# How often attention and norm work is driven between the matmul groups of the output projection: paces 6 and 1 become 3 and 3

## The chip, the cores and the metric

The kernel runs on one Trainium2 chip, as one program on 8 cores. Each core takes 2048 of the 16384 tokens and the whole of every weight matrix; the cores exchange nothing. The metric is the device time of the slowest core in microseconds.

## What is computed

One transformer layer on x of 16384 tokens x 4096. Attention is over the heads of one token: for each token 64 queries, 64 keys and 64 values of width 64 give a 64 x 64 score matrix. The second part is a matmul with bias plus a mixture of 8 rank-16 experts, the top two per token.

```python
def attn(h):                      # h: layernorm(x)
    q, k, v = (h @ W.T).reshape(b, s, 64, 64)       # for Wq, Wk, Wv; q, k, v times head-dim masks
    w = softmax(einsum('bshd,bsgd->bshg', q, k) / 8)
    return einsum('bshg,bsgd->bshd', w, v).reshape(b, s, 4096) @ Wo.T
def ffn(h):
    base = h @ W_base.T + b_base
    rw, sel = top_k(h @ W_router.T, 2); w = onehot-sum of softmax(rw) at sel
    return base + 2 * einsum('ter,te,eor->to', einsum('td,erd->ter', h, A), w, B)
x = x + layernorm(attn(layernorm(x)))
x = x + layernorm(ffn(layernorm(x)))
```

## The kernel before

Each engine's instruction list is written out by hand: a Python function `emit` appends an instruction to one of five lists (tensor, vector, scalar, gpsimd, sync) with the semaphore values it waits for. Each engine works its list strictly in the order in which Python emitted it. DMAs are instructions too: those on the sync list stand on SP's queue, those on the gpsimd list on POOL's, and a DMA that waits holds up all that is behind it on that list.

A core's 2048 tokens are two chunks (`c` = 0, 1) of 1024, and a chunk is eight slices of 128 tokens (`tau`). The transposed activations of a chunk stand in LNT. A projection of a chunk goes over eight blocks of 512 output columns (`n`), each block over eight groups (`ktg`). A group is one weight load of 128 x 2048 bf16 (512 KB, one of four buffers WG) and its matmuls of 128 x 128 by 128 x 512, four per slice. In a half projection with four slices a group has 16 matmuls. After a block, ACT copies the four banks out of PSUM (L601) and POOL writes them to DRAM (apn).

Weights come in two ways. In chunk 0 the first use of a matrix is "cast_save": POOL loads float32 with a cast (1 MB read), and SP then writes the bf16 form to a scratch tensor; the buffer is free for the fourth group after when that save has landed and the matmuls are done. All other uses are "scratch": SP loads the bf16 form (WG<-s_wo).

The stages of a chunk are: layer norm and transposes; the projections q, k, v (written to DRAM); attention for slices 0 to 3, on its own; then the two halves of the wo projection, which the change touches:

- First half (`proj_half` on slices 0 to 3), with the generator `a3_units` for the attention of slices 4 to 7. A slice has two batches of 64 tokens. A batch (`attn_batch`) has one unit that issues eight gathers on SP with 128-byte pieces (QSG, KB, VB), then four waves of six units (Q transposes; K transposes with the QBD copies on DVE; scores with the KTS copies on ACT; maximum, exponentials and P transposes; output matmuls with QBD copies on ACT; normalization into OB on DVE), then one unit that issues the two writes of OB to DRAM on SP. After both batches one unit issues the read-back BFN<-on on POOL, and one transposes BFN into LNT (L278). These are 2 x 26 + 2 = 54 units per slice and 216 in all.
- Second half (`proj_half` on slices 4 to 7, weights from scratch), with the generator `a5_b0_units` for slices 0 to 3. A slice has six units: load of T2 and XT on POOL and a layer norm; the residual add, the xp write and a second layer norm; transposes of BFN; the 32 router matmuls; the top-2 arithmetic on DVE; one matmul and a copy of the router weights (L677, L680). These are 24 units.

After the matmuls of every group `drive(gen, pace)` takes `pace` units from the generator, if it has any, and so puts their instructions behind that group on every list. After the last block `drain` takes what is left with no group between. Then come the rest of the same layer-norm work with the expert part, and the second matrix in two halves.

Of the kernel before, what the change touches and what calls it, by code (L numbers as in the profile page):

```python
# [26 lines left out]
def _build_program():  # L27
# [25 lines left out]
    ap_d = nc.dram_tensor("apn", [CH, DM], F32, kind="Internal").ap()  # L53
# [67 lines left out]
    def emit(eng, fn, waits=(), inc=None, amt=1):  # L121
        w = []
        for s_, v_ in waits:
            assert v_ <= cnt[s_], f"{eng}: wait on future {s_}={v_}>{cnt[s_]}"
            if v_ > seen[eng][s_]:
                seen[eng][s_] = v_
                w.append((s_, v_))
        if inc is not None:
            cnt[inc] += amt
        sched[eng].append((tuple(w), fn, inc, amt))  # L130
        return cnt[inc] if inc is not None else None
# [3 lines left out]
    def g_w(*keys):  # L135
        out = []
        for k in keys:
            out += guards.get(k, [])
        return out

    def g_set(key, *pairs):
        guards[key] = list(pairs)
# [4 lines left out]
    def dma(eng, out, in_, waits=(), sem=None):  # L147
        return emit(eng, lambda e, o=out, i=in_: e.dma_start(out=o, in_=i),  # L148
                    waits, inc=sem, amt=16)
# [90 lines left out]
    def load_wgroup(nm, n, ktg, kind):  # L240
        b = wg_idx[0] % 4
        wg_idx[0] += 1
        waits = g_w(f"WG{b}")
        if kind == "cast_save":
            src = wT[nm].rearrange("(a p) c -> a p c", p=128)[
                4 * ktg:4 * ktg + 4, :, 512 * n:512 * n + 512].transpose([1, 0, 2])
            uv = dma("gpsimd", WG[b][:].rearrange("p (a c) -> p a c", a=4), src, waits,
                     sem=f"wgu{b}")
            rdy = (f"wgu{b}", uv)
            qv = dma("sync", wS[nm][n, ktg], WG[b][:], [rdy], sem=f"sw{b}")  # L250
            g_set(f"WG{b}", (f"sw{b}", qv))
        else:
            rdy = (f"wg{b}", dma("sync", WG[b][:], wS[nm][n, ktg], waits, sem=f"wg{b}"))
            g_set(f"WG{b}")
        return b, rdy

    def wg_done(b, sem, val):
        g_add(f"WG{b}", (sem, val))
# [38 lines left out]
    for c in range(NCH):  # L297
      try:
# [257 lines left out]
        def drive(gen, k):  # L556
            for _ in range(k):
                if next(gen, "END") == "END":
                    return False
            return True  # L560

        def drain(gen):
            for _ in gen:
                pass
# [3 lines left out]
        a35h0_v, a35h0_s = cnt["V"], cnt["S"]  # L568
# [1 line left out]
        ph(4, c)  # L570
        ap_i = [0]

        def proj_half(nm, taus, banks, src, gen, img_d, first_waits=(), pace=3):
            for n in range(NB):
                for ktg in range(8):
                    b, rdy = load_wgroup(nm, n, ktg, src)
                    for k4 in range(4):
                        kt = ktg * 4 + k4
                        for ti, tau in enumerate(taus):
                            waits = []  # L580
                            if k4 == 0 and ti == 0:
                                waits.append(rdy)
                            if ktg == 0 and k4 == 0:
                                waits += g_w(f"bank{banks[ti]}")
                                if n == 0 and ti == 0:
                                    waits += list(first_waits)
                            emit("tensor",
                                 lambda e, kt=kt, tau=tau, b=b, k4=k4, bk=banks[ti],
                                        st=(ktg == 0 and k4 == 0), sp=(ktg == 7 and k4 == 3):
                                 e.matmul(pb(bk, 0, 512),  # L590
                                          LNT[:, colk(kt, tau):colk(kt, tau) + 128],
                                          WG[b][:, k4 * 512:k4 * 512 + 512], start=st, stop=sp),
                                 waits, inc="T" if (k4 == 3 and ti == len(taus) - 1) else None)
                    wg_done(b, "T", cnt["T"])
                    if gen is not None:
                        drive(gen, pace)
                tmm = cnt["T"]
                for ti, tau in enumerate(taus):
                    sl = ap_i[0] % 4
                    ap_i[0] += 1  # L600
                    ev = emit("scalar", lambda e, bk=banks[ti], sl=sl: e.activation(  # L601
                        APST[:, sl * 512:sl * 512 + 512], pb(bk, 0, 512), AF.Copy),
                        ([("T", tmm)] if ti == 0 else []) + g_w(f"APs{sl}"), inc="S")
                    g_set(f"bank{banks[ti]}", ("S", ev))
                    uv = dma("gpsimd", img_d[tau * 128:tau * 128 + 128, 512 * n:512 * n + 512],
                             APST[:, sl * 512:sl * 512 + 512], [("S", ev)], sem=f"ap{sl}")
                    g_set(f"APs{sl}", (f"ap{sl}", uv))

        gen_h1 = a3_units(range(4, 8), 8, (4, 5, 6, 7))
        proj_half("wo", [0, 1, 2, 3], [0, 1, 2, 3], src_kind0, gen_h1, ap_d,  # L610
                  [("V", a35h0_v), ("S", a35h0_s)], pace=6)
        drain(gen_h1)
        g_set("LNTa", ("T", cnt["T"]))
        a4h0_ap = [(f"ap{i}", cnt[f"ap{i}"]) for i in range(4)]
        a4h0_vs = [("V", cnt["V"]), ("S", cnt["S"])]

        def a5_b0_units(taus, tbank):
            for tau in taus:
# [22 lines left out]
                for kt in range(KT):  # L641
# [43 lines left out]

        gen_a5h0 = a5_b0_units(range(0, 4), (0, 1, 2, 3))
        a4h1_ap = [None]
        proj_half("wo", [4, 5, 6, 7], [4, 5, 6, 7], "scratch", gen_a5h0, ap_d, a4h0_vs,
                  pace=1)
        a4h1_ap[0] = [(f"ap{i}", cnt[f"ap{i}"]) for i in range(4)]  # L690
        drain(gen_a5h0)
        g_set("LNTb", ("T", cnt["T"]))
# [188 lines left out]
```

How the kernel before makes its waits and increments, by code:

```python
        def run(eng):  # L827
            for waits, fn, inc, amt in sched[name]:
                for s_, v_ in waits:
                    eng.wait_ge(sems[s_], v_)
                instr = fn(eng)
                if inc is not None:
                    instr.then_inc(sems[inc], amt)
```

## Time and profile before

| | us |
|---|---|
| median of the two timed runs | 8399.7 (8324.7 and 8474.7) |
| the profiled execution, its own time | 8290.5 |
| its span, slowest core (core 2) | 8288.9 |
| spans of the eight cores | 8245.5 to 8288.9 |
| TensorE matmul busy | 5459.9 (66%) |
| DVE busy | 1493.0 (18%) |
| ACT busy | 773.5 (9%) |

The time of one execution is the span of its slowest core plus the little that lies around it, 1.6 us here. Busy time of TensorE counts the matmuls as the trace models them: they are pipelined, so the start of one to the start of the next says more than a duration. The chain that ended last consists for 57% of TensorE, 17% of DMA, 11% of DVE and 6% of ACT work. The mean granted TensorE clock is 0.81 of full speed, as a mean over time at the two levels of 1.2 and 2.4 GHz.

### The profile page before, as it was taken

To read this page: it belongs to the slowest core of one execution; us is meant where nothing else is said; L and a number is where in the kernel's file an instruction comes from. 1 tells how busy PE (TensorE), PEld (TensorE's weight loads), DVE (VectorE), ACT (ScalarE), POOL (GpSimd) and SP (SyncE) were. 2 spreads that over 40 slices of the span, in tenths; PEclk is the share of its full clock that TensorE was granted. 3 is DMA by queue.
4 is the path that set the end of the run, shared out by engine and by line. 5 is a ranking of instruction groups with operands and counts; after the bars stand their busy time and mean duration, and the time that the engine had idled before them with its cause. 6 is when DMAs were issued, how large, how long until landed. Compare 5 with 4: busy or idle time off the path is not lost.

```text
span 8288.9 us, 69958 instructions; the slowest of 8 cores (8245.5 to 8288.9 us)
## 1 busy us (share of the span) xinstructions
PE 5459.9 (66%) x28056; PEld 2571.1 (31%) x28056; DVE 1493.0 (18%) x2144; ACT 773.5 (9%) x1427; POOL 498.9 (6%) x785
## 2 busy tenths in 40 slices
PE   4888888842344568465736888888842556676964
PEld 2333333322222223122313333333322223332321
DVE  4000000023212131401033000000023221414012
ACT  1000000012211100000001000000012221000000
POOL 1000000000000110111100000000000000000110
PEclk7999999965666789688868999999965677887977
DMA  6666666632454675698552222222223334655655
GB/s 148 143 144 141 144 140 140 143 71 51 84 100 96 133 222 177 184 195 225 178 207 89 79 80 82 77 76 76 78 54 54 82 79 113 224 171 172 206 187 190
DMA packets 940079, 1084.79 MB, mean 131 GB/s; under 512 B 575217, under 2 KB 792306, under 8 KB 923378
## 3 DMA queue, kind: packets, MB, share of 16 engines
q0 software_dynamic: 225872, 492.98, 26.3%
q1 hardware_dynamic: 713890, 587.34, 23.4%
q8 instruction: 229, 3.75, 0.2%
q14 instruction: 88, 0.72, 0.0%
HBM read 885.23 MB, written 369.10 MB: 151 GB/s over the span
## 4 chain that ended last, share of the span: by engine, by line
PE 57%; DMA 17%; DVE 11%; ACT 6%; SPq 4%; issue 4%; POOL 1%; DVEq 0%; ACTq 0%; POOLq 0%
PE PALL L341 33%; PE PALL L590 10%; PE PALL L764 8%; SPq L148 4%; DVE BN L192 4%; DMA WG<-wbT 3%; DMA T<-yn 2%; DMA WG<-woT 2%; DMA VB<-vn 2%; ACT QBD L494 2%; ACT PSTG L470 2%; PE PALL L278 1%; DMA T<-apn 1%; PE PALL L487 1%; PE PALL L407 1%
## 5 line engine op out<-in xcount | busy, mean ns | idle before, releaser
L341 PE MATMUL PALL<-WG,LNT 128*128 128x512 bf16 x12288 | 2798.9, 390 | 411.4 <-DVE QST L359 112.7
L341 PEld LDWEIGHTS PALL<-WG,LNT 128*128 128x128 bf16 x12288 | 1224.7, 100 | 1985.1 <-issue 623.0
L590 PE MATMUL PALL<-WG,LNT 128*128 128x512 bf16 x4096 | 1081.4, 428 | 166.2 <-DMA WG<-woT 106.7
L764 PE MATMUL PALL<-WG,LNT 128*128 128x512 bf16 x4096 | 935.1, 390 | 158.3 <-DMA WG<-wbT 146.8
L278 PE MATMUL PALL<-idt,BFN 128*128 128x128 bf16 x1536 | 165.9, 304 | 783.8 <-DVE BFN L204 556.4
L590 PEld LDWEIGHTS PALL<-WG,LNT 128*128 128x128 bf16 x4096 | 434.3, 108 | 772.5 <-issue 421.8
L764 PEld LDWEIGHTS PALL<-WG,LNT 128*128 128x128 bf16 x4096 | 404.5, 100 | 678.4 <-issue 237.0
L192 DVE BATCH_NORM_STATS2 BN<-T 128x6 f32<-128x512 f32 x320 | 193.6, 676 | 1914.5 <-DMA T<-yn 1262.9
L359 DVE TENSOR_TENSOR QST<-PALL,maskK 128x512 bf16<-128x512 f32 x128 | 81.3, 685 | 2067.9 <-PE PALL L341 2022.5
L278 PEld LDWEIGHTS PALL<-idt,BFN 128*128 128x128 bf16 x1536 | 154.8, 143 | 796.1 <-issue 795.0
L435 ACT ACTIVATE KTS<-PALL 128x512 bf16<-128x512 f32 x192 | 104.2, 595 | 2960.2 <-PE PALL L427 2960.2
L407 PE MATMUL PALL<-idt,QSG 128*128 128x128 bf16 x1024 | 104.4, 274 | 402.9 <-DMA VB<-vn 374.3
L416 DVE CAST QBD<-PALL 128x512 bf16<-128x512 f32 x256 | 162.0, 685 | 629.7 <-PE PALL L407 629.7
L359 DVE TENSOR_TENSOR QST<-PALL,maskV 128x512 bf16<-128x512 f32 x128 | 81.0, 685 | 990.8 <-PE PALL L341 950.6
L487 PE MATMUL PALL<-idt,PSTG 128*128 128x128 bf16 x1024 | 104.5, 274 | 219.6 <-ACT PSTG L470 219.6
L407 PEld LDWEIGHTS PALL<-idt,QSG 128*128 128x128 bf16 x1024 | 88.3, 126 | 421.2 <-issue 415.3
L470 ACT ACTIVATE PSTG<-PALL,NM 64x512 bf16<-64x512 f32 x256 | 167.6, 679 | 212.9 <-DVE NM L461 122.0
L481 DVE TENSOR_REDUCE ZW<-PSTG 128x8 f32<-128x1024 bf16 (+1 forms) x96 | 151.3, 1576 | 199.6 <-ACT PSTG L470 199.6
L290 DVE CAST LNT<-PALL 128x512 bf16<-128x512 f32 x192 | 132.3, 692 | 285.9 <-PE PALL L278 285.5
L148 POOL DMA_DIRECT2D BFN<-on x16 | 8.6, 536 | 2763.1 <-DMA on<-OB 2718.1
L777 PE MATMUL PALL<-bbn,onesb 1*128 1x512 bf16 x128 | 51.4, 401 | 186.6 <-DMA bbn<-bb 186.6
L786 ACT ACTIVATE APST<-PALL 128x512 f32<-128x512 f32 x128 | 76.2, 597 | 1035.2 <-PE PALL L781 1031.2
(99 smaller groups left out, 2166.7 us busy)
## 6 DMA issues: line engine op xcount, KB each, us to landing
WG<-s_wo SPq DMA_DIRECT2D x192, 512.0 KB, 3.9
WG<-s_wb SPq DMA_DIRECT2D x192, 512.0 KB, 3.6
XT<-x POOLq DMA_DIRECT2D x24, 2048.0 KB, 12.3
WG<-wqT POOLq DMA_DIRECT2D x64, 512.0 KB, 5.7
s_wq<-WG SPq DMA_DIRECT2D x64, 512.0 KB, 2.8
WG<-wkT POOLq DMA_DIRECT2D x64, 512.0 KB, 5.7
s_wk<-WG SPq DMA_DIRECT2D x64, 512.0 KB, 3.1
WG<-wvT POOLq DMA_DIRECT2D x64, 512.0 KB, 5.7
```

The lines of the kernel that those rows point to most:

```text
L148: return emit(eng, lambda e, o=out, i=in_: e.dma_start(out=o, in_=i), waits, inc=sem, amt=16)
L192: emit("vector", lambda e, i=i: e.bn_stats(BN[:, 6 * i:6 * i + 6], src_ap[:, 512 * i:512 * i + 512]), (list(vwaits) + g_w("MV") + g_w("BN" ...
L278: emit("tensor", lambda e, bk=bk, kt=kt, off=off: e.matmul(pb(bk, off * 128, 128), src_sb[:, kt * 128:kt * 128 + 128], idt[:], start=True, ...
L341: e.matmul(pb(tau, 0, 512), LNT[:, colk(kt, tau):colk(kt, tau) + 128], WG[b][:, k4 * 512:k4 * 512 + 512], start=st, stop=sp),
L359: ev = emit("vector", lambda e, tau=tau, sl=sl, mk=mk: e.tensor_tensor(QST[:, sl * 512:sl * 512 + 512].rearrange("p (h d) -> p h d", d=64) ...
L407: emit("tensor", lambda e, j=j, jj=jj, p=p, qb_bk=qb_bk: e.matmul(pb(qb_bk[j // 4], (j % 4) * 128, 128), QSG[p][:, jj * 128:jj * 128 + 128 ...
L416: emit("vector", lambda e, pw=pw, bk=bk, i_=i_: e.tensor_copy(QBD[pw][:, i_ * 512:i_ * 512 + 512], pb(bk, 0, 512)), [("T", t_s0)] if i_ == ...
L470: s_s6 = emit("scalar", lambda e, a=a, pw=pw, bk_i=bk_i, sb_=s_bk[bk_i]: e.activation(PSTG[pw][64 * a:64 * a + 64, bk_i * 1024:bk_i * 1024 ...
L487: emit("tensor", lambda e, j=j, pw=pw, ptb=pt_bk[j // 4], po=(j % 4) * 128: e.matmul(pb(ptb, po, 128), PSTG[pw][:, j * 128:j * 128 + 128], ...
L494: emit("scalar", lambda e, pw=pw, bk=bk, i_=i_: e.activation(QBD[pw][:, i_ * 512:i_ * 512 + 512], pb(bk, 0, 512), AF.Copy), [("T", t_s7)] ...
L590: e.matmul(pb(bk, 0, 512), LNT[:, colk(kt, tau):colk(kt, tau) + 128], WG[b][:, k4 * 512:k4 * 512 + 512], start=st, stop=sp),
L764: e.matmul(pb(bk, 0, 512), LNT[:, colk(kt, tau):colk(kt, tau) + 128], WG[b][:, k4 * 512:k4 * 512 + 512], start=st, stop=False), waits,
```

## The change

Two numbers change. In the first half of the wo projection, three attention units are driven after each group and no longer six. In the second half, three norm and router units are driven after each group and no longer one. The parameter `pace` is gone, and the 3 that was its default is written in place. No instruction is added or removed; their order on the engines' lists is another.

```diff
-        def proj_half(nm, taus, banks, src, gen, img_d, first_waits=(), pace=3):
+        def proj_half(nm, taus, banks, src, gen, img_d, first_waits=()):
...
                     if gen is not None:
-                        drive(gen, pace)
+                        drive(gen, 3)
...
         proj_half("wo", [0, 1, 2, 3], [0, 1, 2, 3], src_kind0, gen_h1, ap_d,
-                  [("V", a35h0_v), ("S", a35h0_s)], pace=6)
+                  [("V", a35h0_v), ("S", a35h0_s)])
...
-        proj_half("wo", [4, 5, 6, 7], [4, 5, 6, 7], "scratch", gen_a5h0, ap_d, a4h0_vs,
-                  pace=1)
+        proj_half("wo", [4, 5, 6, 7], [4, 5, 6, 7], "scratch", gen_a5h0, ap_d, a4h0_vs)
```

## Rows read from the trace of the kernel before

**Rows 1.** Stretches: busy us (instructions) per engine, granted clock, DMA share, GB/s.

```profile
2139.00:2811.00 672.00, 292.91 (x1984) 150.15 (x1984) 142.02 (x208) 130.32 (x224) 37.81 (x56) 0.67 0.48 94
2811.00:2976.00 165.00, 109.36 (x450) 45.15 (x451) 0.11 (x1) 8.68 (x17) 25.90 (x39) 0.86 0.95 201
2976.00:3307.00 331.00, 248.87 (x1283) 115.88 (x1281) 99.92 (x160) 29.00 (x64) 23.45 (x42) 0.88 0.57 199
6466.00:6994.00 528.00, 287.44 (x1985) 147.74 (x1986) 141.58 (x208) 130.19 (x224) 10.69 (x20) 0.72 0.35 85
6994.00:7100.00 106.00, 99.94 (x452) 43.97 (x451) 0.57 (x1) 8.86 (x18) 7.82 (x15) 0.99 0.52 168
7100.00:7427.00 327.00, 247.64 (x1284) 115.93 (x1281) 99.91 (x160) 29.00 (x64) 23.38 (x42) 0.87 0.61 205
```

**Rows 2.** Timeline, TensorE, chunk 1, first batch: start, duration, instruction, idle before.

```profile
6498.16 0.61 PE L407 MATMUL PALL<-idt,QSG 128*128 128x128 bf16 x8
...
6500.42 0.39 PE L446 MATMUL PALL<-KTS,QBD 128*128 128x64 bf16 x8 [1.43 <-ACT KTS L435]
6503.23 0.61 PE L487 MATMUL PALL<-idt,PSTG 128*128 128x128 bf16 x8 [2.41 <-ACT PSTG L470]
...
6505.56 6.27 PE L590 MATMUL PALL<-WG,LNT 128*128 128x512 bf16 x16
```

**Rows 3.** Timeline, TensorE, chunk 1, second half: eight groups of one block.

```profile
7280.29 28.61 PE L590 MATMUL PALL<-WG,LNT 128*128 128x512 bf16 x128 [0.89 <-ACT APST L601]
```

**Rows 4.** Groups by line, TensorE, 6466 to 6994: busy us, mean ns, idle before.

```profile
L590 PE MATMUL PALL<-WG,LNT 128*128 128x512 bf16 x577 | 201.9, 524 | 4.4 <-ACT APST L601 3.6 <-ACT LNT L292 0.8
...
L278 PE MATMUL PALL<-idt,BFN 128*128 128x128 bf16 x128 | 14.3, 310 | 55.0 <-DMA BFN<-on 55.0
```

**Rows 5.** Timeline, TensorE, chunk 1, second batch: the Q transposes.

```profile
6557.60 0.61 PE L407 MATMUL PALL<-idt,QSG 128*128 128x128 bf16 x8 [1.12 <-DVE OB L520]
```

**Rows 6.** Timeline, chunk 1, TensorE and SP's queue, where a slice begins.

```profile
6598.42 4.24 PE L590 MATMUL PALL<-WG,LNT 128*128 128x512 bf16 x16
...
6600.08 2.98 SPq L148 DMA_DIRECT2D WG<-s_wo  x4
```

**Rows 7.** Second batch's load: SP's queue, landing of its WG loads, TensorE's Q.

```profile
6520.19 1.63 SPq L148 DMA_DIRECT2D on<-OB  x2
...
6531.91 2.71 SPq L148 DMA_DIRECT2D WG<-s_wo  x4
...
DMA to landing us min/median/max: 5.5/5.9/7.0
...
6535.13 1.01 PE L407 MATMUL PALL<-idt,QSG 128*128 128x128 bf16 x8 [9.72 <-DMA VB<-vn]
```

**Rows 8.** Timeline, TensorE: groups right after a short gap, chunk 0 and chunk 1.

```profile
2960.16 8.75 PE L590 MATMUL PALL<-WG,LNT 128*128 128x512 bf16 x32 [2.58 <-DMA WG<-woT]
...
7099.64 10.52 PE L590 MATMUL PALL<-WG,LNT 128*128 128x512 bf16 x48 [2.36 <-ACT APST L601]
```

**Rows 9.** Timeline, TensorE, chunk 0: first load, block's end, second load.

```profile
2164.47 1.01 PE L407 MATMUL PALL<-idt,QSG 128*128 128x128 bf16 x8 [21.21 <-DMA VB<-vn]
...
2280.71 5.83 PE L590 MATMUL PALL<-WG,LNT 128*128 128x512 bf16 x16 [11.51 <-DMA WG<-woT]
...
2399.84 1.01 PE L407 MATMUL PALL<-idt,QSG 128*128 128x128 bf16 x8 [11.42 <-DMA VB<-vn]
```

**Rows 10.** Timeline, chunk 1, second half and just behind it: TensorE, then DVE.

```profile
7141.69 3.57 PE L278 MATMUL PALL<-idt,BFN 128*128 128x128 bf16 x32 [31.53 <-DVE BFN L204]
...
7263.80 3.57 PE L278 MATMUL PALL<-idt,BFN 128*128 128x128 bf16 x32 [14.19 <-DVE BFN L204]
...
7476.61 0.27 PE L677 MATMUL PALL<-idt,WBF 128*8 128x128 bf16 x1 [3.52 <-DVE WBF L672]
...
7157.23 4.83 DVE L192 BATCH_NORM_STATS2 BN<-T 128x6 f32<-128x512 f32 x8
...
7177.18 2.41 DVE L204 TENSOR_SCALAR BFN<-XT,NMR,RSTD 128x4096 bf16<-128x4096 f32 x1
```

## The prediction, made before the changed kernel had run

> **What bounds the kernel now.** I read the stretches first [rows 1]. A chunk has two stretches that the edit touches: the first half of the wo projection, with attention units driven between its matmul groups, and the second half, with the layer-norm and router units driven between them. In chunk 0 these are 672 + 165 = 837 us and 331 us; in chunk 1, 528 + 106 = 634 us and 327 us. That is 2129 of 8289 us, and only these can move directly. TensorE is the engine to watch: it takes all of this work in one order, and every stall sits in its queue. In the attention part it is busy about half the time at a granted clock of 0.67 to 0.72; afterwards, with groups alone, it is busy 0.99 of the time in chunk 1 with DVE idle, and in chunk 0 the DMA engines are at 0.95 of their time. So in chunk 0 the leftover groups wait for weights, in chunk 1 they run at full speed, and no group is left to cover an attention stall.
>
> Then I read TensorE's own order of instructions in chunk 1 [rows 2]. One wave of attention is five steps, Q and K transposes, scores S, P transposes, output O. With pace 6 one group stands between O and the next Q. The stalls are 1.43 us before S, 2.41 before P, 1.33 before O: Q's start to the next group's start is 6505.56 - 6498.16 = 7.4 us. Groups are long too. 16 matmuls take 28.61 / 8 = 3.6 us at the 2.4 GHz level [rows 3], but 6.27 in the row shown, and 201.9 / 36 = 5.6 in the mean of the stretch's 36 [rows 4]. They start at the lower clock after the wave. In a slice's second batch the group falls between S and P, which hides the 2.41, but leaves 1.33, 1.12 (Q on DVE's OB) and 1.43 [rows 2, 5].
>
> **What the first edit does.** A slice of attention has 54 units: 26 for each batch (a load unit, four waves of six, a write unit) and two for reading the result back. Four slices are 216. Pace 6 spends them in 36 groups and leaves 28 bare. Pace 3 puts 18 groups in each slice, 192 units in 64 groups, and 24 units (last slice, from P of its fifth wave on) are drained with no group. Place by place, per slice, first in chunk 1:
>
> First batch, units 2 to 25. After Q and K comes a group, then S P O, then a group. The 1.43 before S is hidden. S to the next group's start is 6505.56 - 6500.42 = 5.1 us. Q and K take 0.9 with nothing to wait for. The group after Q and K follows straight on a running one, so 3.6; the group after S P O follows 3.7 us of stalls in 5.1, and I keep 5.6. Sum: first group 4.2 [rows 6], Q and K 0.9 + 0.5 wait, second group 3.6, four times (5.1 + 5.6) = 42.8, three times (0.9 + 3.6) = 13.5: 65.5.
>
> Second batch. Its output writes and loads stand on SP's queue, and the next weight loads behind them. SP begins at 6520.19, issues 12 us of writes and gathers, gets to the weights at 6531.91 and these land 5.9 later, at 6537.8. The Q transposes at 6535.13 waited 9.72 for the gathers after a group of 6.3 [rows 7], so O ended at 6519.1 and the weights come 18.7 after it. Now the next group stands behind S, just in time. At pace 3 the units 25 to 27 hold no TensorE work, so two groups stand there, but the second one's weights are the ones behind the gathers: it can't start before 18.7. The wait is 18.7 - 5.6 = 13.1, that group 5.6 after the pause; the edit makes this place worse by 3. The same at the first load of a slice: those weights are issued at 6600.08 and come about 6606, where Q and K would end at 6604.2 (6598.42 + 4.24 + 0.5 + 0.9) [rows 6], a wait of 1.8. The rest is dense: Q K S is 6500.42 + 0.39 - 6498.16 = 2.65, P O is 6505.56 - 6503.23 = 2.3, four of each 19.8, and eight groups. Between them lie only gaps of 1.3 to 1.4 us. For the clock the rows say: three groups after a gap of 2.36 us ran at 10.52 = 3.5 each, two after 2.58 us at 8.75 = 4.4 each [rows 8]. So gaps of 1.4 keep the upper level; I take 3.6, with 2.0 once for warming: 30.8. TensorE waits 55.0 / 4 = 13.7 us for a slice's read-back after O [rows 4], of which the group after unit 51 hides 3.6: 10.1; the transposes take 3.4. Sum with the 1.8: 13.1 + 5.6 + 19.8 + 30.8 + 10.1 + 3.4 + 1.8 = 84.6.
>
> A slice is 150 us. Three are 450; the last runs to unit 30, 65.5 + 1.8 + 13.1 + 5.6 + 2.65 = 88.7. The drain: P and O 4.9, three waves of 7.4 + 1.2, read-back 13.7 + 3.4: 47.8. Total 587 against 634: **47 us saved**. Nine groups more per slice cost 18 us there, against 33 us bare.
>
> Chunk 0 differs in that weights come by POOL with a cast and are saved by SP [rows 9]. The gathers wait for that save, so Q waits 21.2 at a slice's start and its next group starts cold (5.6). The second batch's Q waits 11.42 after a group of 6.4, so it starts 17.8 after O; here both groups have their weights already, so 17.8 - 5.6 - 3.6 = 8.6. A block's end costs 11.5 to 13.9, since the next weights stand behind the result writes on POOL; there are seven, and they stay seven: one of them, after the eighth group, now falls on the gathers' wait and I count 7 for it, 12 for the others. A slice: 4.2 + 21.2 + 1.4 (Q and K at the lower clock) + 5.6 + 42.8 + 13.5 = 88.7; then 8.6 + 3.6 + 11.3 (three times 2.65, once 3.3) + 9.3 + 30.8 + 10.4 + 5 (transposes and the weights behind the read-back) = 79. Three are 503; block ends 67 + 12; last slice 88.7 + 8.6 + 3.6 + 3.3 = 104; drain 48; small waits for weights in the dense part 10. Total 744 against 837: **93 saved**. Most is the 165 us of bare groups at 5.9 each, paced by DMA, which go behind attention. DMA work allows it: 0.48 x 672 / 4 = 81 us per slice, plus nine groups at 0.95 x 165 / 28 = 5.6, gives 131 of about 184 us.
>
> The Trainium skill (DMA: Bandwidth & Descriptors, Issuing engines are not separate DMA queues) says that transfers from all issuing engines run on the same 16 DMA engines and interleave. By that, the doubled weight traffic lengthens the gathers. The rows bear it out mildly: gathers are ready 17.8 us after O in chunk 0 with cast loads beside them, about 16 in chunk 1. If each of the two gathers of a slice took 2 us more, the sum would lose 14 us a chunk.
>
> **What the second edit does.** A slice has 6 units, four slices 24. Pace 1 spreads them over 24 groups, pace 3 over 8. The transposes wait for a DVE chain: two layer norms and an add, 7157.23 to 7179.6, 22.4 us [rows 10]. Now slices are 7263.80 - 7141.69 = 122.1 over three, 40.7 each, since three groups lie between the transposes and the next chain's start on DVE. At pace 3 that is 3.4 transposes, a group 3.6, router matmuls about 1, a bare wait for the router weights 3.5, then 0.6: 12.1, and with 22.6 for the chain 34.7. The first chain starts earlier: the last result writes have landed during the drain, and the T2 load is issued right behind the read-back, so I put the first transposes 26 us after the stage's start where they stand 42 after it now (7099.64 to 7141.69). Total 26 + 3 x 34.7 + 12.1 + seven blocks of 29.5 = 348.7 against 327: **21 lost** in each chunk. Bounds: with the chain period unchanged and no earlier start, 16 groups uncovered, 59; with PE-side savings complete, 10.
>
> **Sum.** 47 + 93 - 42 = 98 saved: 8290.5 - 98 = 8193. This is against the profiled execution's own time; the two timed runs stand 0.4% and 2.2% above it (8324.7 and 8474.7, median 8399.7).
>
> **The rivals.** *The clock stays down between the groups.* If the eight dense groups and the four after Q and K ran at 5.6 too, each costs 2.0 more: 12 x 2.0 x 3.5 slices x 2 chunks = 168 lost, hence 8193 + 168 = 8361, slower than before. For it: every one of the 36 groups now starts below full speed after stalls of 1.1 to 2.4 us. Against: those stalls add up to 3.9 us or more before a group, and here to 1.4. It decides at 98 / 84 = 1.2 us per group, a mean of 4.8 us in these places. *The clock stays up everywhere.* If the groups after S P O also run at 3.6, 4 x 2.0 x 3.5 x 2 = 56 more saved, 8137. For it: the low stretch shrinks from 7.4 us with Q and K to 5.1; in the row shown P still runs at the upper level. *The second edit pays in full.* 59 instead of 21 in each chunk: 8269. For it, ACT's evacuation of a block stands behind the chain; against, now all units end inside the first block. *Weights run short in chunk 0.* The bare groups' 5.9 us for 64 groups and 27 us of attention transfers per slice make a floor of 486 us, well under 744; only the small waits could grow, to some 30 us: 8213, which I count to the forecast.
>
> **How the numbers follow.** Forecast (8193, own range 8160 to 8230) 0.5; clock up everywhere 0.2; second edit in full 0.12; clock down 0.1; rest, spread either way, 0.08. The range 8080 to 8320 takes in 8137 with as much again, 8269 and half of the clock rival, and leaves out the rest. Two per cent, about what a measurement of this kernel can tell from no change, is 166 us. Faster by more needs the warm rival and something more, 0.15; slower by more needs the cold one and something more, 0.04; the same 0.81.
>
> **What would show it.** Right: between 2.4 GHz groups the stretch from Q K to the next group shows groups of 3.6; a second-batch group waits about 13 us for WG from s_wo in chunk 1, just after O; the first half lasts 740 to 750 us in chunk 0 and 580 to 590 in chunk 1; 24 units run without a group at its end; all router work lies in the first 8 groups of the second half, 34.7 us apart, then 29.5 us blocks; the second half 345 to 352. Wrong: dense groups at over 4.8 us, gathers that take over 20 us, or a first transposition in the second half that still comes 40 us in.

## The result, and the profile after

The change makes the kernel 1.0% faster: the ratio of its time to that of the kernel before is 0.9897, with a 95% interval of 0.9882 to 0.9911. By the measure of 2% that is no change, as forecast; the 86 us that the ratio stands for compare with the 98 of the sum. The median over all 12 executions is 8387.5 us against 8403.4 before: in seven of the 12 (8321.5 to 8777.8 us) one or both dies ran TensorE at a lower granted clock, as happens to the kernel before too, and all other times here are of the other executions, or of cores on a die to which this did not happen. The profiled execution took 8229.8 us (8290.5 before), its slowest core was core 7.

The four stretches that answer to [rows 1] are these, in the same columns (start and end in the span, length, busy us of TensorE, weight loads, DVE, ACT and POOL, granted clock, DMA share, GB/s):

```profile
2139.00:2890.00 751.00, 367.53 (x2434) 187.59 (x2435) 142.03 (x208) 139.01 (x240) 65.47 (x98) 0.73 0.66 135
2890.00:3235.00 345.00, 252.53 (x1284) 117.77 (x1281) 99.96 (x160) 29.40 (x65) 20.25 (x38) 0.86 0.51 178
6407.00:7006.00 599.00, 358.78 (x2432) 181.62 (x2430) 142.03 (x208) 138.88 (x240) 20.30 (x38) 0.80 0.41 110
7006.00:7355.00 349.00, 253.74 (x1284) 118.81 (x1284) 99.96 (x160) 29.73 (x66) 20.22 (x38) 0.86 0.54 182
```

| stretch | before | by the prediction | after |
|---|---|---|---|
| chunk 0, first half | 837 | 744 | 751 |
| chunk 0, second half | 331 | 352 | 345 |
| chunk 1, first half | 634 | 587 | 599 |
| chunk 1, second half | 327 | 349 | 349 |
| together | 2129 | 2032 | 2044 |

So 85 us are gained in these stretches: 121 in the first halves, 36 given back in the second. The granted clock of the first halves rose a little: before it was 0.67 and 0.86 in the two parts of chunk 0, 0.71 as a mean over time, and 0.72 and 0.99 in those of chunk 1, 0.77 as a mean; now it is 0.73 and 0.80. No part with bare groups is left in them. The spans of the two traces differ by 61 us and not by 85, since the rest of the program took 24 us longer here. Nor is one core all cores: in this same execution the first half of chunk 0 lasts 733 to 751 us from core to core and that of chunk 1 587 to 603, and core 7 is at or near the upper end of both. (The half is taken here from its first group to the first group behind its last read-back.)

TensorE's timeline in chunk 1, first batch and then second batch, answers to [rows 2] and [rows 5] (start, duration, instruction, idle before and who ended it):

```profile
6441.56 3.63 PE L590 MATMUL PALL<-WG,LNT 128*128 128x512 bf16 x16
...
6447.84 0.61 PE L487 MATMUL PALL<-idt,PSTG 128*128 128x128 bf16 x8 [2.41 <-ACT PSTG L470]
6449.77 0.59 PE L506 MATMUL PALL<-VB,QBD 128*128 128x64 bf16 x8 [1.33 <-ACT QBD L494]
6450.17 6.33 PE L590 MATMUL PALL<-WG,LNT 128*128 128x512 bf16 x16
...
6488.36 5.99 PE L590 MATMUL PALL<-WG,LNT 128*128 128x512 bf16 x16 [15.04 <-DMA WG<-s_wo]
...
6496.45 0.39 PE L446 MATMUL PALL<-KTS,QBD 128*128 128x64 bf16 x8 [1.43 <-ACT KTS L435]
6496.68 3.62 PE L590 MATMUL PALL<-WG,LNT 128*128 128x512 bf16 x16
...
6502.07 0.39 PE L506 MATMUL PALL<-VB,QBD 128*128 128x64 bf16 x8 [1.33 <-ACT QBD L494]
6502.30 3.62 PE L590 MATMUL PALL<-WG,LNT 128*128 128x512 bf16 x16
...
6531.14 0.39 PE L446 MATMUL PALL<-KTS,QBD 128*128 128x64 bf16 x8 [1.43 <-ACT KTS L435]
6532.43 6.12 PE L590 MATMUL PALL<-WG,LNT 128*128 128x512 bf16 x16 [0.89 <-ACT APST L601]
```

The group after Q and K takes 3.63 us, the one after S P O still 4.8 to 6.3. In the second batch six groups in a row take 3.62, though a gap of 1.33 or 1.43 us stands before and behind each. The two exceptions there are the group behind the long wait (5.99) and the one that begins a block: ACT's copies out of PSUM put a second gap of 0.89 us behind the 1.43 before S, and it takes 6.12. The one long wait is for weights, 15.04 us in the middle of the slice, as the queue order of [rows 7] had it. SP's queue at that place:

```profile
6466.64 2.90 SPq L148 DMA_DIRECT2D on<-OB  x2
6469.59 6.11 SPq L148 DMA_DIRECT2D QSG<-qn  x2
...
6482.95 11.79 SPq L148 DMA_DIRECT2D WG<-s_wo  x5
```

The weights are issued 16.3 us after the writes of OB, behind eight gathers. In chunk 0 the rows that answer to [rows 9], TensorE first and then SP's queue between its second and third row:

```profile
2164.28 1.01 PE L407 MATMUL PALL<-idt,QSG 128*128 128x128 bf16 x8 [21.60 <-DMA VB<-vn]
...
2234.30 9.97 PE L590 MATMUL PALL<-WG,LNT 128*128 128x512 bf16 x32 [13.92 <-DMA WG<-woT]
2264.31 1.01 PE L407 MATMUL PALL<-idt,QSG 128*128 128x128 bf16 x8 [20.04 <-DMA VB<-vn]
```

```profile
2234.12 0.32 SPq L148 DMA_DIRECT2D s_wo<-WG  x1
2234.53 9.06 SPq L148 DMA_DIRECT2D on<-OB  x2
2243.68 7.71 SPq L148 DMA_DIRECT2D QSG<-qn  x2
```

And in chunk 1's second half, for [rows 10], the first two transposes and the first block without units:

```profile
7031.25 3.57 PE L278 MATMUL PALL<-idt,BFN 128*128 128x128 bf16 x32 [21.36 <-DVE BFN L204]
...
7066.27 3.57 PE L278 MATMUL PALL<-idt,BFN 128*128 128x128 bf16 x32 [17.90 <-DVE BFN L204]
...
7147.54 30.06 PE L590 MATMUL PALL<-WG,LNT 128*128 128x512 bf16 x128 [0.89 <-ACT APST L601]
```

The transposes come 25 us after the half's start at 7006.3 and the next lie 35.0 us later, as worked out (26 and 34.7).

### The profile page after: what moved, and what is told of

Its sections match the earlier page's. It is cut to its first block, busy times and chain, and to the rows that moved or that the text cites. A ratio compares the mean times of both kernels' runs of the same rounds, so it can differ in the third digit from the quotient of the medians.

```text
span 8228.2 us, 69958 instructions; the slowest of 8 cores (8151.4 to 8228.2 us)
## 1 busy us (share of the span) xinstructions
PE 5400.6 (66%) x28056; PEld 2555.5 (31%) x28056; DVE 1491.4 (18%) x2144; ACT 774.2 (9%) x1427; POOL 496.2 (6%) x785
## 4 chain that ended last, share of the span: by engine, by line
PE 58%; DMA 15%; DVE 11%; ACT 6%; SPq 5%; issue 4%; POOL 1%; DVEq 0%; ACTq 0%; POOLq 0%
PE PALL L341 33%; PE PALL L590 11%; PE PALL L763 8%; SPq L148 5%; DVE BN L192 4%; DMA WG<-wbT 3%; DMA T<-yn 3%; ACT QBD L494 2%; ACT PSTG L470 2%; DMA VB<-vn 1%; PE PALL L278 1%; PE PALL L487 1%; DMA WG<-woT 1%; PE PALL L407 1%; DMA T<-apn 1%
## 5 line engine op out<-in xcount | busy, mean ns | idle before, releaser
L590 PE MATMUL PALL<-WG,LNT 128*128 128x512 bf16 x4096 | 1040.2, 415 | 182.5 <-DMA WG<-woT 93.3
```

The source lines that it names most:

```text
L590: e.matmul(pb(bk, 0, 512), LNT[:, colk(kt, tau):colk(kt, tau) + 128], WG[b][:, k4 * 512:k4 * 512 + 512], start=st, stop=sp),
```

## The experiments

All edits are shown against the kernel before, with the parts left out marked by `...`. From the third experiment on the paces are 3 and 3, as in the changed kernel, where nothing else is said.

**Each edit alone.** The theory says that they pull against each other. The first edit alone:

```diff
-                  [("V", a35h0_v), ("S", a35h0_s)], pace=6)
+                  [("V", a35h0_v), ("S", a35h0_s)], pace=3)
```

> Pace 3 in the first half, 1 in the second. Theory (the stage sums of the changed kernel's trace: first halves 85 and 34 us shorter, second halves 14 and 21 longer, of which the earlier start of the norm chain already gives back some 16 in each): the first halves as in the changed kernel, about 750 and 600 us, and the second halves 313 us each instead of 331 and 327, since transposes come 28 us in instead of 42. Together 147 us less than before, ratio 0.982. Rival (the second halves are untouched by the first edit; the drain gives them nothing): 119 us less, ratio 0.986, second halves 331 and 327.

It took 8162.7 us where the kernel before took 8304.8 and 8314.7 on the same chip: 0.982, from one execution. The windows of core 6 in the traced execution, which is another one, first and second half of each chunk:

```profile
2135.00:2870.00 735.00, 365.33 (x2432) 187.16 (x2432) 142.14 (x209) 139.00 (x241) 65.50 (x98) 0.73 0.65 137
2870.00:3179.00 309.00, 250.34 (x1284) 116.52 (x1284) 99.98 (x161) 29.36 (x65) 21.62 (x38) 0.90 0.58 200
6328.00:6940.00 612.00, 365.10 (x2432) 183.35 (x2430) 141.93 (x208) 138.67 (x240) 20.31 (x38) 0.79 0.41 108
6940.00:7251.00 311.00, 247.52 (x1284) 115.73 (x1284) 100.11 (x161) 29.50 (x66) 21.60 (x38) 0.91 0.60 204
```

The second halves take 309 and 311 us with pace 1, less than the 331 and 327 before: the first edit's drain gives them a head start for the norm chain. The rival, that they are untouched, falls. The first halves show how far one core of one trace can be trusted: 735 and 612 here where the same code in the changed kernel had 751 and 599.

The second edit alone:

```diff
         proj_half("wo", [4, 5, 6, 7], [4, 5, 6, 7], "scratch", gen_a5h0, ap_d, a4h0_vs,
-                  pace=1)
+                  pace=3)
```

> Pace 6 in the first half, 3 in the second. Theory: without the drain in front the first transposes come 42 us in, then three slices of 34.4, 12 and seven blocks of 29.5: 364 us where it was 327 to 331, so 35 us lost in each chunk, 70 in all, ratio 1.0085, and the first halves unchanged at 837 and 634. Rival (all 16 groups bare at 3.7): 59 in each, ratio 1.014.

It took 8386.8 us, 1.009 of before, one execution again. TensorE's timeline, start of chunk 1's second half:

```profile
7099.47 3.61 PE L590 MATMUL PALL<-WG,LNT 128*128 128x512 bf16 x16 [2.36 <-ACT APST L601]
7136.27 3.23 PE L278 MATMUL PALL<-idt,BFN 128*128 128x128 bf16 x32 [33.19 <-DVE BFN L204]
```

One group and then 33 us of waiting, where before three groups lay ahead of the transposes. From 7099.5 to the half's end at 7457.7 are 358 us, 31 more than before; in chunk 0 it is 364, 33 more. The theory's 35 holds, the rival's 59 doesn't. On these whole times, one execution each, the first edit is worth about 147 us and the second costs about 77, of which 64 lie in the two second halves of the core shown; together 70, near the 86 measured for both.

**Where the mid-slice wait comes from.** The load of the next group is put on SP's queue before the units driven after this one, in the halves with scratch weights.

```diff
-                    b, rdy = load_wgroup(nm, n, ktg, src)
+                    b, rdy = nxt if nxt is not None else load_wgroup(nm, n, ktg, src)
...
                     wg_done(b, "T", cnt["T"])
+                    nxt = None
+                    if src == "scratch" and gen is not None and n * 8 + ktg < 63:
+                        nxt = load_wgroup(nm, (n * 8 + ktg + 1) // 8, (ktg + 1) % 8, src)
                     if gen is not None:
                         drive(gen, pace)
```

> Paces 3 and 3; where weights come by SP from scratch, the load of the next group is put on SP's queue before the units driven after this group, and no longer behind them. It touches the first half of chunk 1 and the second halves. Theory (the 13 to 15 us wait for WG in the middle of a slice is the place behind the gathers on SP's queue): the wait moves to the Q transposes and shrinks to about 7 us after two groups, the second group of a slice waits for nothing; some 11 us per slice, chunk 1's first half from 599 to about 562, ratio about 0.985 against before. Rival (the weights are late because the DMA engines are busy with the gathers, wherever they stand): chunk 1's first half stays within 8 us of 599, ratio 0.990.

Measured: 8211.2 us, 0.988 of before. TensorE's timeline on core 0, chunk 1, the place where core 7 of the changed kernel waited 15.04 us:

```profile
6484.79 9.76 PE L591 MATMUL PALL<-WG,LNT 128*128 128x512 bf16 x32 [0.89 <-ACT APST L605]
6503.70 1.01 PE L407 MATMUL PALL<-idt,QSG 128*128 128x128 bf16 x8 [9.16 <-DMA VB<-vn]
```

Both groups now run together, and Q waits 9.16 (about 7 expected). The first half of chunk 1 takes 564 us on this core and 560 to 572 over all eight, where the changed kernel had 587 to 603: core by core 22 to 39 us less, 30 in the mean, against the 37 of the theory and the 8 at most of the rival. The order on the queue made the wait; the weights themselves are there in time beside the gathers. The whole kernel gained some 20 us on the changed one (0.985 of before was expected), from a single execution.

**What the clock level is worth.** A slice is cut so that the groups fall after S and after O in both batches.

```diff
-                        drive(gen, pace)
+                        drive(gen, pace[(n * 8 + ktg) % len(pace)] if isinstance(pace, list) else pace)
...
-                  [("V", a35h0_v), ("S", a35h0_s)], pace=6)
+                  [("V", a35h0_v), ("S", a35h0_s)],
+                  pace=[4] + [3] * 7 + [5] + [3] * 8)
```

> Paces 3 and 3, but in the first half a slice is cut 4, seven times 3, 5, eight times 3, so that in both batches the groups fall after S and after O. Theory (the clock level between the groups is worth as much as the stalls that they hide): all groups but those after a gather or read-back wait run at 3.6 us; chunk 1's first half from 599 to about 540, chunk 0's from 750 to about 720; ratio 0.979. Rival (only stalls count, groups after S P O gain nothing when S stands before them): about 4 us per slice, 15 per chunk, ratio 0.986.

> The kernel of aligned once more, for a trace on an undisturbed die: by the clock theory chunk 1's first half is about 540 us with groups after S and after O at 3.6 us in both batches; by the rival about 585 with the groups of the first batch at 5 us.

It took 8167.6 and, in the second run, 8124.9 us: 0.983 and 0.980 of before. The trace of the second run, core 3: first its windows of the first halves, then a stretch of chunk 1's first batch.

```profile
2135.00:2870.00 735.00, 342.19 (x2433) 178.31 (x2434) 142.14 (x208) 139.04 (x240) 65.51 (x98) 0.74 0.66 136
6368.00:6907.00 539.00, 331.20 (x2434) 173.19 (x2432) 142.15 (x208) 139.06 (x240) 20.32 (x38) 0.84 0.46 123
```

```profile
6445.16 0.39 PE L506 MATMUL PALL<-VB,QBD 128*128 128x64 bf16 x8 [1.33 <-ACT QBD L494]
6445.47 3.61 PE L590 MATMUL PALL<-WG,LNT 128*128 128x512 bf16 x16
...
6451.18 0.39 PE L446 MATMUL PALL<-KTS,QBD 128*128 128x64 bf16 x8 [1.43 <-ACT KTS L435]
6451.41 3.62 PE L590 MATMUL PALL<-WG,LNT 128*128 128x512 bf16 x16
```

Chunk 1's first half is 539 us (540 expected; 527 to 539 over all cores), and the groups take 3.6 except those that begin a block or follow a pause (up to 6.2). To see how the 60 us divide, the groups by line of chunk 1's first half: first the changed kernel, then this one.

```profile
L590 PE MATMUL PALL<-WG,LNT 128*128 128x512 bf16 x1024 | 282.6, 436 | 70.1 <-DMA WG<-s_wo 62.7 <-ACT APST L601 6.2 <-ACT LNT L292 0.8
L487 PE MATMUL PALL<-idt,PSTG 128*128 128x128 bf16 x256 | 21.5, 232 | 49.9 <-ACT PSTG L470 49.9
L407 PE MATMUL PALL<-idt,QSG 128*128 128x128 bf16 x256 | 20.7, 227 | 5.1 <-DVE OB L520 3.5 <-DMA VB<-vn 1.4 <-PE PALL L590 0.2
...
L446 PE MATMUL PALL<-KTS,QBD 128*128 128x64 bf16 x256 | 13.2, 197 | 22.8 <-ACT KTS L435 22.8
```

```profile
L590 PE MATMUL PALL<-WG,LNT 128*128 128x512 bf16 x1024 | 258.3, 407 | 9.7 <-ACT APST L601 6.3 <-DMA WG<-s_wo 1.1 <-ACT LNT L292 0.8
L407 PE MATMUL PALL<-idt,QSG 128*128 128x128 bf16 x256 | 21.5, 233 | 55.4 <-DMA VB<-vn 53.8 <-DVE OB L520 1.1 <-PE PALL L590 0.4
L487 PE MATMUL PALL<-idt,PSTG 128*128 128x128 bf16 x256 | 20.3, 224 | 6.2 <-ACT PSTG L470 6.2
...
L446 PE MATMUL PALL<-KTS,QBD 128*128 128x64 bf16 x256 | 13.7, 200 | 45.5 <-ACT KTS L435 45.5
```

The groups themselves give 24 us (282.6 to 258.3), which is clock; the wait before P gives 44 and the one before S takes back 23; the mid-slice wait only changes its name from WG to VB, 62.7 to 53.8. So the clock is worth about as much as the hidden stalls, and the rival, which allowed 15 us, falls.

In chunk 0 the theory failed: 735 us on this core and not 720, and over all cores 730 to 738 where the changed kernel already had 733 to 751, 5 us less in the mean. The Q transposes there, first in the changed kernel and then in this one:

```profile
L407 PE MATMUL PALL<-idt,QSG 128*128 128x128 bf16 x256 | 23.9, 249 | 125.7 <-DMA VB<-vn 122.3 <-DVE OB L520 3.4
L407 PE MATMUL PALL<-idt,QSG 128*128 128x128 bf16 x256 | 23.1, 243 | 164.1 <-DMA VB<-vn 163.0 <-DVE OB L520 1.1
```

TensorE saved the same things as in chunk 1 (19 us in the groups, 44 before P, less 23 before S), and the wait for gathers grew by 41: the gathers came no earlier, so TensorE only stood longer in front of them.

**Chunk 0.** The save of a group's weights is put behind the driven units on SP's queue.

```diff
+                    late = [] if gen is not None else None
+                    b, rdy = load_wgroup(nm, n, ktg, src, late)
...
                     if gen is not None:
                         drive(gen, pace)
+                    for sv in late or []:
+                        sv()
```

> Paces 3 and 3; in chunk 0's first half the save of a group's weights is put on SP's queue behind the units driven after the group and no longer ahead of them. Theory (at a slice's start the Q transposes wait 22, 22, 17 and 9 us since the gathers stand on SP behind a save that waits for weights which POOL could only ask for after the read-back): these four waits go to under 5 us each, the ones in the middle of a slice from 20 and 15 to about 8, and chunk 0's first half goes from 750 to about 670. Rival (the gathers are slow in chunk 0 because cast loads share the DMA engines): the waits stay within 3 us of what they are, 750 stays.

By what was said with the result, this kernel has no whole time to compare, only cores of its trace. On core 5 the first half of chunk 0 takes 703 us (670 expected; the same core had 742 in the changed kernel). The four waits of Q at a slice's start are 10.4, 12.7, 9.6 and 5.9 us where they were 21.6, 22.4, 16.9 and 9.2, and the first two in a slice's middle 11.9 and 11.3 where they were 20.0 and 15.1. All Q waits for gathers together make 77.4 us where core 7 of the changed kernel had 122.3; core 7 of this run has 71.2 and also 703 us. So the order on the queue was some 40% of it, more than the rival allows and less than the theory said. Part of the remainder is SP's own issuing. SP's queue around the first gathers, first here and then in the changed kernel:

```profile
2118.45 4.42 SPq L148 DMA_DIRECT2D QSG<-qn  x2
2122.97 22.74 SPq L148 DMA_DIRECT2D KB<-kn  x4
```

```profile
2138.91 9.55 SPq L148 DMA_DIRECT2D QSG<-qn  x2
2148.56 8.74 SPq L148 DMA_DIRECT2D KB<-kn  x4
```

Started early, the gathers stand beside the read-back and the four cast loads behind it, and issuing the four KB gathers takes SP 22.74 us instead of 8.74. So the rival has its part too.

**Weights three groups ahead.** Both halves ask for weights three groups ahead of the matmuls, and the saves stand behind the driven units. `prefetch(k)` puts all loads up to group k on their queues and keeps their saves in a list.

```diff
+            prefetch(3)
...
-                    b, rdy = load_wgroup(nm, n, ktg, src)
+                    b, rdy = wq_[n * 8 + ktg]
...
                     wg_done(b, "T", cnt["T"])
+                    prefetch(n * 8 + ktg + 3)
                     if gen is not None:
                         drive(gen, pace)
+                    if saves[n * 8 + ktg] is not None:
+                        saves[n * 8 + ktg]()
```

> Paces 3 and 3; both halves ask for weights three groups ahead of the matmuls, and saves stand behind the driven units. Theory (in chunk 0 the seven block ends cost 13 us each because the next weights stand behind the result writes on POOL, and the mid-slice waits come from SP's order): chunk 0's first half from 750 to 570 to 600 us, chunk 1's from 599 to about 555, ratio about 0.966. Rival (chunk 0 is bound by the DMA engines themselves, so waits only move): chunk 0's first half not under 680, ratio 0.98 or more.

It took 8028.3 to 8059.6 us in three executions against 8291.5 and 8293.8: 0.971, from 0.968 to 0.972 over all pairs. The group of the matmuls in chunk 0's first half (2133 to 2753 on core 1, 620 us):

```profile
L607 PE MATMUL PALL<-WG,LNT 128*128 128x512 bf16 x1027 | 280.3, 433 | 9.2 <-ACT APST L621 6.2 <-DMA WG<-woT 1.4 <-ACT LNT L299 0.8
```

The wait for woT is 1.4 us where the changed kernel had 93.3: the waits at block ends came of loading too late, behind the result writes on POOL, and are gone. 620 (614 to 624 over all cores) is above the 570 to 600 expected, since 75 us of waits for gathers remain. Chunk 1 has 568 (555 expected), no less than with weights one group ahead.

**All of it.** Weights three groups ahead, late saves, the gathers of a batch issued one batch ahead (in the attention stage without groups too), the cut of the aligned kernel, and pace 1 in the second half. The edit beyond those shown is in the batch generator:

```diff
+            if (tau, bt) == ahead[0]:
+                issue_gathers(tau, bt)
+            nx = ahead.index((tau, bt)) + 1
+            if nx < len(ahead):
+                issue_gathers(*ahead[nx])
```

> Weights three groups ahead and late saves; gathers of a batch issued one batch ahead, in both attention stages; the first half cut 4, seven times 3, 5, eight times 3; pace 1 in the second half. Theory (stalls before Q are queue order, the clock stays up when S stands before the group, pace 1 covers the norm chain): chunk 1's first half about 480 us, chunk 0's about 510, second halves about 312, the attention stage without groups some 70 us shorter per chunk; ratio 0.92 to 0.94. Rival (transfers collide once nothing waits, the read-back and the weights take longer): first halves above 560 each, ratio 0.95 or more.

It took 7641.1 to 7653.5 us in three executions against 8291.5 and 8293.8: 0.922, from 0.921 to 0.923 over all pairs. The windows of core 3:

```profile
2056.00:2602.00 546.00, 326.83 (x2432) 171.41 (x2432) 142.13 (x208) 139.10 (x241) 65.41 (x98) 0.84 0.90 182
2602.00:2913.00 311.00, 249.24 (x1284) 116.09 (x1284) 99.92 (x160) 29.02 (x64) 21.62 (x38) 0.89 0.57 200
6006.00:6468.00 462.00, 307.15 (x2433) 166.35 (x2434) 142.14 (x208) 139.07 (x240) 20.31 (x38) 0.92 0.54 140
6468.00:6777.00 309.00, 246.11 (x1284) 115.11 (x1282) 99.91 (x160) 29.00 (x64) 21.59 (x38) 0.91 0.58 205
```

Chunk 1's first half takes 462 us (480 expected), chunk 0's 546 (510 expected): there the DMA engines are at 0.90 of their time, which points at the transfers as the next limit, though no run tests that. Of the 645 us gained, 501 lie in these stretches (2129 to 1628). The rest lies outside them: the attention stage ahead of the first half now ends 79 us earlier in chunk 0 (at 2056 against 2135 on the same core of the aligned kernel).

## Why the prediction was right or wrong

*The mechanism and its size were right.* Faster by about 1%, inside 2%, with 93 and 47 us gained and 42 given back: measured 86 (837 - 751), 35, and 36. The likeliest case was the one that came.

*The step that failed is the base on which the number and its range stand.* "This is against the profiled execution's own time; the two timed runs stand 0.4% and 2.2% above it". I saw the two, put what stands above the profiled execution at nothing, and drew 8080 to 8320 from the bounds of the costs alone. The median of all executions, 8387.5, lies outside it, 194 us above the 8193. Of these, some 154 are the reason given with the result, of which the 8474.7 was a sign: the five executions that it leaves are at 8230 to 8237, inside the range. The other 40 are about 29 of base and 12 of gain: the five like executions of the kernel before have a median of 8319 and not the 8290.5 of its profiled one, and 86 us were gained and not 98. The spread of the measurement belonged into the range as a term of its own.

*First edit, chunk 1.* Term by term: slices of 153, 150 and 150 us where 150 was the sum. The group behind the gathers waited 15.0, 13.7, 15.4 and 13.6 us (13.1), the second group of a slice 1.4 to 1.9 (1.8). Dense groups were 3.62 (3.6). The step that was short is the drain. "three waves of 7.4 + 1.2" was taken from waves that follow a group; without groups every instruction ran at the lower clock (eight Q transposes took 1.01 us and not 0.61), and a wave took 9.8 us (Q to Q, 6958.89 to 6968.70). The 12 us by which 599 exceeds 587 are 9 from the last slice and 3 from the first. Of the 9 the three waves are 3 to 4; the rest are the first P of the drain, which waited 3.8 us and not 2.4, a read-back wait of 15.0 and not 13.7, and small pieces.

*First edit, chunk 0.* The step that failed is "one of them, after the eighth group, now falls on the gathers' wait and I count 7 for it". They did not overlap. The group waited 13.92 for its weights and Q another 20.04 after both groups, 34 us where 15.6 were counted. The writes of OB and the gathers stand on SP behind the save of those very weights, which went out at 2234.12, and from there to Q at 2264.31 are 30 us where the prediction reads 17.8 from O to Q in the batch of [rows 9]: SP took 9.06 us to issue the two writes and 7.71 for the first two gathers, where the kernel before took 1.64 and 3.60 in that batch. The experiment with late saves shows the first part of the chain: with the saves out of the way Q waits 11.9 there and not 20.0. The second slice has no block end at this place and still waited 15.1 where 8.6 were counted, 24 us from O to Q; "gathers that take over 20 us", which I had named as a sign of being wrong, did come in two slices.

That the sum for chunk 0 came within 7 us is in part luck. The four waits in the middle of a slice made 66 us (34.0, 15.1, 10.1, 7.0) where 41 were counted. The four at a slice's start made 70 (21.6, 22.4, 16.9, 9.2) where 85 were, and the 10 us for small waits did not come. The slices took 203, 199, 189 and 160 us where the sum has 187, 192, 192 and 164 besides these 10. And 751 is the slowest of the eight cores.

*Second edit.* The chain of 34.7 us per slice came as 34.7 in chunk 1 and 34.1 in chunk 0, the first transposes 25 and 23 us in (26). The loss was 22 and 14 (21 each). That the head start belongs to the first edit and not to the second is shown by the two single edits: 309 to 311 us with pace 1 behind a drain, 358 and 364 with pace 3 without one.

*The rivals.* "The clock stays down between the groups" is refuted by the 3.62 of the dense groups. "The clock stays up everywhere" is refuted by groups of 4.8 to 6.3 after S P O. "The second edit pays in full" falls with 358. "Weights run short in chunk 0" did not show apart from the block ends. Gathers do get slower beside other transfers: in the late-save run SP needs 22.7 us for issuing four of them, which took 3.9 in a place of the kernel before with none of these loads about. That is in line with the Trainium skill (DMA: Bandwidth & Descriptors, Issuing engines are not separate DMA queues), by which transfers of all issuing engines share the same DMA engines, though no run here shows whether the engines or the issue are the tight place. In the changed kernel's own chunk 0 the two long cases, 30 and 24 us against 17.8, are 18 us; that it was these other transfers that slowed them there was not tested by itself.

## What to carry to other kernels

When work is interleaved on in-order queues, ask of each driven unit which DMA issues it puts ahead of the next load, on every queue: here such order cost 30 us in chunk 1's first half (596 to 566 as a mean of the eight cores) and 123 in chunk 0's (741 to 617). Load ahead of the driven units and store behind them. Place big matmul groups so that no more than one short stall stands before each: two (2.41 and 1.33 us, or 1.43 and 0.89) brought them to the lower clock here. Where a queue of loads sets the pace, as in chunk 0, time saved on TensorE only lengthens its wait (122 to 163 us for the gathers). And give a long chain on another engine as many groups as it takes, not as few as possible. State a forecast's range with the spread of the measurement in it.

## What the runs showed of the hardware

Groups of 16 matmuls kept the 2.4 GHz level with gaps of 1.3 to 1.4 us before and behind them, over six groups in a row, but after S P O with gaps of 2.41 and 1.33 us they began at the lower level in the changed kernel (4.7 to 6.3 us instead of 3.6), and so they did at a block's start with gaps of 1.43 and 0.89 (5.1 to 6.1). SP needed 3.9 us to issue four gathers of 128-byte pieces in one place of the kernel before, 8.7 in the changed kernel beside a save and cast loads, and 22.7 in the late-save run beside the read-back and four cast loads: the time to issue such gathers went with what else was in flight.
